# The chunked scan of a delta-rule attention with its operands and evictions laid out the other way round

## What is computed

```python
q, k, v = short_conv(x @ Wq.T), short_conv(x @ Wk.T), short_conv(x @ Wv.T)   # 4 taps, silu
q, k = l2norm(q), l2norm(k)
v, kb = v * beta, k * beta                 # chunks of 32 tokens, 8 a sequence
A = where(tri, 0, -kb @ k.T)               # T = inverse of (1 - A), row by row
u, w = T @ v, T @ kb
def step(S, (qi, ki, ui, wi)):             # over the 8 chunks in order
    attn = where(tri_s, 0, qi @ ki.T)
    u_i = ui - wi @ S
    o = qi @ S + attn @ u_i
    S = S + ki.T @ u_i
# paths = (3-tap filter of v, 63-tap filter of v, o, v); a small network on their
# means and variances gives softmax weights; out = norm(weighted sum) @ Wo.T
x = x + out
gate, value = x2 @ W11[e], x2 @ W12[e]     # x2 = layernorm(x), e over 8 experts
y = x + sum over the top 2 of score * ((gate * sigmoid(gate) * value) @ W2[e])
```

## Time and profile before

| what | number |
|---|---|
| median of the runs shown | 401.59 us (397.64 to 405.42, 3 runs) |
| the profiled execution | 399.36 us |
| its span | 397.5 us |
| TensorE busy (matmul) | 338.5 us, 85% |
| VectorE busy | 275.7 us, 69% |
| ScalarE busy | 139.4 us, 35% |
| GpSimd busy | 88.2 us, 22% |

### The profile page before, as it was taken

The page is one execution under the profiler, slowest core; times in us unless marked ns, Lnnn a source line. Parts: engine busy times, 40 slices in busy tenths (PEclk is TensorE's granted clock), DMA queues, the critical chain, the costliest instruction groups (busy, mean ns, idle before and its releaser), DMA issues.

```text
span 397.5 us, 14307 instructions
## 1 busy us (share of the span) xinstructions
PE 338.5 (85%) x6364; PEld 254.6 (64%) x6364; DVE 275.7 (69%) x679; ACT 139.4 (35%) x257; POOL 88.2 (22%) x152
## 2 busy tenths in 40 slices
PE   6989986966884679888989779989889999889997
PEld 6344974645433566755766557768767668668886
DVE  2889963256828874977765599779736969859654
ACT  2243614130352224354512613544252454242221
POOL 6463000061445234400201423702100000300000
PEclk9899889885597578999999998999989999978999
DMA  7331443001111011110000103020000000000000
GB/s 242 157 107 28 110 75 115 5 3 31 17 13 28 4 30 17 16 27 2 3 2 2 31 3 44 0 41 5 2 28 4 4 0 2 1 0 5 23 2 26
DMA packets 42668, 12.47 MB, mean 31 GB/s; under 512 B 35440, under 2 KB 41712, under 8 KB 42480
## 3 DMA queue, kind: packets, MB, share of 16 engines
q1 hardware_dynamic: 39440, 9.47, 11.1%
q10 hardware_dynamic: 3168, 2.10, 1.7%
HBM read 8.68 MB, written 2.88 MB: 29 GB/s over the span
## 4 chain that ended last, share of the span: by engine, by line
PE 60%; DVE 21%; issue 7%; ACT 5%; POOL 3%; DMA 2%; SPq 0%; DVEq 0%; ACTq 0%
PE ps L592 18%; PE ps L486 13%; PE ps L635 11%; PE ps L531 9%; PE ps L516 4%; DVE v_room L1266 2%; DMA late_sb<-in_late 2%; DVE x L1285 2%; POOL g L430 1%; PE ps L667 1%; PE ps L659 1%; PE ps L686 1%; DVE pmean L1317 1%; DVE toep_room L1318 1%; DVE toep_room L1369 1%
## 5 line engine op out<-in xcount | busy, mean ns | idle before, releaser
L635 PE MATMUL ps<-w_sb,v_room 128*128 128x128 f32 x512 | 64.3, 280 | 4.3 <-DVE v_room L1266 2.2
L635 PEld LDWEIGHTS ps<-w_sb,v_room 128*128 128x128 f32 x512 | 62.1, 195 | 8.8 <-DVE v_room L1266 4.3
L592 PE MATMUL ps<-x_hi,w_sb 128*128 128x512 f32 x128 | 61.0, 477 | 5.3 <-issue 1.9
L1266 DVE TENSOR_TENSOR v_room<-toep_room,ps 128x512 f32<-128x512 f32 x64 | 43.3, 682 | 30.3 <-PE ps L592 16.0
L885 ACT ACTIVATE toep_room<-ps 128x512 f32<-128x512 f32 x64 | 38.0, 596 | 66.1 <-PE ps L592 56.9
L592 PE MATMUL ps<-x_lo,w_sb 128*128 128x512 f32 x128 | 52.5, 410 | 0.0
L592 PE MATMUL ps<-x_hi,w_lo 128*128 128x512 f32 x128 | 52.4, 410 | 0.0
L1285 DVE SCALAR_TENSOR_TENSOR x<-ps,rs,x 128x128 f32<-128x128 f32 x128 | 35.9, 342 | 10.2 <-PE ps L635 9.9
L396 POOL TENSOR_TENSOR rn<-ss,mh 128x16 f32<-128x16 f32 x8 | 23.1, 2902 | 64.9 <-DVE ss L1106 64.9
L430 POOL TENSOR_TENSOR g<-gm,mh 128x16 f32<-128x16 f32 x4 | 11.6, 2906 | 105.5 <-DVE gm L1386 105.5
L592 PEld LDWEIGHTS ps<-x_hi,w_sb 128*128 128x128 f32 x128 | 25.1, 196 | 14.7 <-DVE v_room L1266 3.8
(11 more groups left out here) (202 smaller groups left out, 582.1 us busy)
## 6 DMA issues: line engine op xcount, KB each, us to landing
toep_room<-in_toep SPq DMA_DIRECT2D x1, 1536.0 KB, 12.6
a_d<-a_hc SPq DMA_DIRECT2D x4, 256.0 KB, 3.0
v_room<-in_w SPq DMA_DIRECT2D x1, 1024.0 KB, 5.7
t<-t_d SPq DMA_DIRECT2D x4, 256.0 KB, 3.0
v_room<-in_w ACTq DMA_DIRECT2D x1, 1024.0 KB, 6.1
taps_room<-in_taps SPq DMA_DIRECT2D x1, 768.0 KB, 6.3
x_sb<-in_x SPq DMA_DIRECT2D x1, 768.0 KB, 9.4
out_y<-x ACTq DMA_DIRECT2D x3, 256.0 KB, 2.4
```

The costliest lines, as they stand in the source:

```text
L592: ins = pe.matmul(bank[:, :], a[cols].bitcast(F32R), c[:, :].bitcast(F32R), start=(k == 0), stop=(k == 2))
L635: ins = pe.matmul(yb[:, P * j:P * j + P], fu[:, e % 2, f, P * j:P * j + P], w2_sb[:, FC * e + f, :], start=(f == 0), stop=(f == FC - 1))
L1266: dve.tensor_tensor(fu[:, e % 2, f, :], sg[:, i % 2, :], ps[VALUE[bank_of(p, i)]][:, :], ALU.mult).then_inc(s["fu_ready"], 1)
```

## The change

Every product of the scan is turned round, so that what was moving is stationary. Stationary are now vb, s_sb and u_sb, 32 columns each; the operands that went in as stationary are moving and lie side by side, so that one product serves several of them:

- vb against t32_t, 32 columns: the first part of u, transposed. It no longer waits for s_ready; that wait stands behind it.
- s_sb against by_s, 96 columns: wneg_t, q_t and a block named carry. carry is the 32 x 32 identity, so its 32 columns give s itself, transposed.
- u_sb against by_u, 64 columns: attn_t and kn, the output's second part and the state's new part.

The three results U, O and S of a step lie side by side in one bank, 96 columns for each of two sequences, and the bank alternates between ps2 and ps4. S is not added up over the scan in PSUM any more: every step adds the carried s and its new part.

The results come out transposed, so they are transposed as they leave PSUM. VectorE does that: a transpose of 128 x 64 in blocks of 32 x 32 for u (L1493 in the new numbering), one for s (L1498), and one for each step's output, straight into delta_hc (L1500). ScalarE's copies of u, s and delta are gone. VectorE's transposes of u and s stand between its lists, where ScalarE's copies stood between ScalarE's.

The identity block is made once at the start: VectorE folds the 128 x 128 identity to id32 and copies it 16 times into carry. In the tables, norm in list 6 of SCAN becomes norm_k in list 6, norm_q in list 7 and norm_kb in list 14, and the second weight split moves from list 0 of SCAN to the end of START. NEXT_START and NEXT_SCAN stay.

The core of the diff:

```diff
         [("q_silu", 0), ("q_hc", 0), ("qk_sq", 0), ("norms", 0)],
         [("router", 1), ("beta", 0), ("tanh", 0), ("beta_hc", 0), ("dstore", 0)],
         [("gate", 0), ("sig", 0), ("value", 0), ("fuse", 0)],
-        [("gate", 1), ("sig", 1), ("value", 1), ("fuse", 1), ("norm", 0), ("gate", 2)],
-        [("sig", 2), ("value", 2), ("gate", 3), ("fuse", 2)], [("g", 0), ("weigh", 0)], [("g", 1), ("mask", 0)],
+        [("gate", 1), ("sig", 1), ("value", 1), ("norm_k", 0), ("fuse", 1), ("gate", 2)],
+        [("sig", 2), ("value", 2), ("gate", 3), ("norm_q", 0), ("fuse", 2)], [("g", 0), ("weigh", 0)], [("g", 1), ("mask", 0)],
         [("sig", 3), ("value", 3), ("fuse", 3), ("centre", 0)],
         [("y", 0), ("square", 0), ("add", 0), ("centre", 3)], [("gate", 4), ("sig", 4), ("value", 4), ("spread", 0), ("fuse", 4)],
-        [("gate", 5), ("square", 3), ("sig", 5), ("value", 5), ("spread", 3)], [("fuse", 5)],
+        [("gate", 5), ("square", 3), ("sig", 5), ("value", 5), ("spread", 3)], [("fuse", 5), ("norm_kb", 0)],
         [("gate", 6), ("centre", 1), ("sig", 6), ("value", 6), ("square", 1)]]
 TAIL = [("delta", 0), ("centre", 2), ("spread", 1), ("square", 2), ("y", 1), ("gate", 7), ("sig", 7),
         ("value", 7), ("hidden_x", 0), ("spread", 2), ("stats", 0), ("fuse", 6), ("gate", 8), ("sig", 8),
...
     if rest and not any(what == "g" for what, _ in items):
         items.append(rest.pop(0))
 assert not rest
-START = [("split", 0), *START[:START.index(("y_out", 0)) + 1], ("reload", 0), *START[START.index(("y_out", 0)) + 1:]]
-SCAN[0].append(("split", 1))
+START = [("split", 0), *START[:START.index(("y_out", 0)) + 1], ("reload", 0), *START[START.index(("y_out", 0)) + 1:],
+         ("split", 1)]
 
 LAST_SCAN = [[item for item in items if item not in (("centre", 1), ("square", 1))] for items in SCAN]
 LAST_SCAN[13].append(("centre", 1))
...
         a_it, t_it, prod = sb("a_it", HB, HB), sb("t_it", HB, HB), sb("prod", HB * HB // 4)
         t16 = sb("t16", M, C)
 
-        kn, q_t, attn_t = (taps_room[:, TOK * k:TOK * k + TOK].rearrange("p (m c) -> p m c", c=C) for k in range(3))
+        by_u = taps_room[:, 0:2 * TOK].rearrange("p (m c) -> p m c", c=2 * C)
+        by_s = sb("by_s", M, 3 * C)
+        attn_t, kn = (by_u[:, :, C * k:C * k + C] for k in range(2))
+        wneg_t, q_t, carry = (by_s[:, :, C * k:C * k + C] for k in range(3))
+        id32 = sb("id32", C)
+
         vb = sb("vb", M, DH)
         t16_t, y_sb = sb("t16_t", M, C), sb("y_sb", M, C)
-        t32_t, wneg_t = sb("t32_t", M, C), sb("wneg_t", M, C)
+        t32_t = sb("t32_t", M, C)
         u_sb, s_sb = sb("u_sb", 2, DH), sb("s_sb", 2, DH)
         delta_hc = sb("delta_hc", M, DH)
         psq = sb("psq", NP, M, DH)
...
         ps = [ctx.enter_context(nc.psum_tensor(f"ps{i}", [P, 512], F32)) for i in range(8)]
         GATE, VALUE, YB, LAST_HALF = (5, 0), (6, 1), 7, 2
 
+        U_COL, O_COL, S_COL, COLS = 0, C, 2 * C, 3 * C
+
+        def scanned(n):
+
+            return ps[(2, 4)[n % 2]]
+
+        def slots(n, col):
+            return scanned(n)[:, 0:2 * COLS].rearrange("p (k c) -> p k c", k=2)[:, :, col:col + C]
+
         FIR = (2, 3, 5, 6)
 
 
...
                     if t is not None:
                         held()
                         if n == 0:
+                            pe.wait_ge(s["carry_ready"], 2)
                             pe.wait_ge(s["w_ready"], t1)
                             pe.wait_ge(s["vb_ready"], t1)
                             pe.wait_ge(s["moved"], t1)
-                        else:
-                            pe.wait_ge(s_ready[n - 1], t1)
                         for k in range(2):
                             m = k * NC + n
-                            ins = heads(ps[4], DH * k, DH, lambda q: t32_t[q, m, :], lambda q: vb[q, m, :],
-                                        start=True, stop=(n == 0))
-                            if n:
-                                ins = heads(ps[4], DH * k, DH, lambda q: wneg_t[q, m, :], lambda q: s_sb[q, k, :],
+                            ins = heads(scanned(n), COLS * k + U_COL, C, lambda q: vb[q, m, :], lambda q: t32_t[q, m, :],
+                                        start=(k == 0), stop=(n == 0))
+                        if n:
+                            pe.wait_ge(s_ready[n - 1], t1)
+                            for k in range(2):
+                                m = k * NC + n
+                                ins = heads(scanned(n), COLS * k, 3 * C, lambda q: s_sb[q, k, :], lambda q: by_s[q, m, :],
                                             start=False, stop=True)
                         ins.then_inc(s["u_done"], 1)
                     run(scan[2 * n])
                     if t is not None:
                         held()
                         pe.wait_ge(u_ready[n], t1)
-                        if n < NC - 1:
-                            for k in range(2):
-                                m = k * NC + n
-
-                                ins = heads(ps[3], DH * k, DH, lambda q: kn[q, m, :], lambda q: u_sb[q, k, :],
-                                            start=(n == 0 and k == 0), stop=(n == NC - 2))
-                            ins.then_inc(s["s_done"], 1)
                         for k in range(2):
                             m = k * NC + n
-                            if n:
-                                heads(ps[2], DH * m, DH, lambda q: q_t[q, m, :], lambda q: s_sb[q, k, :],
-                                      start=True, stop=False)
-                            ins = heads(ps[2], DH * m, DH, lambda q: attn_t[q, m, :], lambda q: u_sb[q, k, :],
-                                        start=(n == 0), stop=True)
-                        ins.then_inc(s["o_done"], 1)
+                            ins = heads(scanned(n), COLS * k + O_COL, 2 * C, lambda q: u_sb[q, k, :], lambda q: by_u[q, m, :],
+                                        start=False, stop=True)
+                        ins.then_inc(s["s_done"], 1)
                     run(scan[2 * n + 1])
                 run(behind)
 
...
-                def delta(_):
-                    if t is not None:
-                        act.wait_ge(s["o_done"], t * NC + NC)
-                        act.activation(delta_hc[:, :, :], ps[2][:, :].rearrange("p (m d) -> p m d", m=M),
-                                       ACT.Copy).then_inc(s["delta_ready"], 1)
-
...
                     return store(b)
                 ahead, scan, behind = lists(t)
                 run(ahead)
-                for n in range(NC):
-                    if t is not None:
-
-                        act.wait_ge(s["u_done"], t * NC + n + 1)
-                        if n:
-                            act.wait_ge(s["o_done"], t * NC + n)
-                        act.activation(u_sb[:, :, :], ps[4][:, 0:2 * DH].rearrange("p (b d) -> p b d", b=2),
-                                       ACT.Copy).then_inc(u_ready[n], 1)
-                    run(scan[2 * n])
-                    if t is not None and n < NC - 1:
-
-                        act.wait_ge(s["s_done"], t * (NC - 1) + n + 1)
-                        if n:
-                            act.wait_ge(s["o_done"], t * NC + n + 1)
-                        act.activation(s_sb[:, :, :], ps[3][:, 0:2 * DH].rearrange("p (b d) -> p b d", b=2),
-                                       ACT.Copy).then_inc(s_ready[n], 1)
-                    run(scan[2 * n + 1])
+                for items in scan:
+                    run(items)
                 run(behind)
 
             pipeline(body)
...
             for j in range(NT):
                 ins = dve.tensor_scalar(xn[:, j, :], x_sb[:, j, :], mv_first[:, j, 0:1], st[:, 2, j:j + 1], ALU.subtract, ALU.mult)
             ins.then_inc(s["xn_ready"], 1)
+            dve.wait_ge(s["pool_consts"], PADS_READY)
+            dve.tensor_reduce(id32[:, :], ident[:, :].rearrange("p (h j) -> p j h", h=H), AX.X, ALU.add).then_inc(s["carry_ready"], 1)
+            dve.wait_ge(s["carry_ready"], 1)
+            dve.tensor_copy(carry, id32[:, :].unsqueeze(1).to_broadcast([P, M, C])).then_inc(s["carry_ready"], 1)
             dve.wait_ge(s["early_loaded"], 32)
             dve.wait_ge(s["late_loaded"], 16)
             scaled(wkc, wk_sb, 1)
...
                     return run(ALONE)
                 ahead, scan, behind = lists(t)
                 run(ahead)
-                for items in scan:
-                    run(items)
+                for n in range(NC):
+                    if t is not None:
+                        dve.wait_ge(s["u_done"], t * NC + n + 1)
+                        dve.transpose(u_sb[:, :, :], slots(n, U_COL)).then_inc(u_ready[n], 1)
+                    run(scan[2 * n])
+                    if t is not None:
+                        dve.wait_ge(s["s_done"], t * NC + n + 1)
+                        if n < NC - 1:
+                            dve.transpose(s_sb[:, :, :], slots(n, S_COL)).then_inc(s_ready[n], 1)
```

(5 more changed lines are left out.)

12 lines of the change are left out of this document (6 added, 6 removed).

## The result

The changed kernel takes 426.4 us (median of 4 runs, 423.6 to 427.6) against 402.0 before: 1.0635 times as long, 95% interval 1.0528 to 1.0742. Forecast was 412 with a range to 420, so the direction was right and the size was about half.

The account below looks back on a forecast made before the run. In the scans TensorE and VectorE, both nearly full, were taken to share the limit. 5 + 5 + 2 + 1.7 - 1 = 12.7 us on 399.4 gave about 412; likeliest range 406 to 418, 8-in-10 range 395 to 420.

Parts of the forecast that it names:

- The order matters more than the price: In the scans, u, s and output wait behind whatever VectorE has queued, and TensorE behind them; transposes' own work 19 us.
- Price of a transpose, 0.21: Each 128x64 transpose on VectorE takes 0.21 us, ends 0.18 and 0.42; 92 of them add 19 us of work.
- Shorter products, 0.18 us a step: TensorE's middle scan step falls from 0.93 to 0.75 us, 5 us over 28 steps.
- the saving counts: Rival: VectorE reaches transposes in time, leaving shorter steps, fewer delta waits and one pause less: 389 us; chance 0.14.
- Scan 2, +5: Early transposes delay the normalisation and first fuse, some 2.9 us; s of step 4 behind the router's weights, about 2 more.
- Scan 4, +5: s of step 4 waits behind the router's weights until 308.1 at least; TensorE passes the last step some 6 us later.
- 13 transposes: Scan 4, weights to the long filter's centring: VectorE has no real pause, so these add 13 x 0.21 us.
- Scan 3, +2: Router's weights cost nothing as TensorE stood still; u of step 5 waits 0.84 us for masks, six late transposes cost more.
- Scan 1, +1.7: At its end the last u waits behind VectorE's variances and seven joining transposes, delaying the next pair's key convolutions 1.7 us.
- One pause fewer, -1: In the scans, a seventh fewer TensorE instructions removes one of the "issue" pauses of about 2 us, taken as -1.
- The clock as a rival: Rival: new waits lower the clock in scans 2 and 4, products grow 7 us: 419; chance 0.12, shared with dear transpose.
- a dear transpose: Rival: each VectorE transpose takes 0.42 us, 19 us more work, half on the path: 422; chance 0.12, shared with falling clock.

Follow-up runs that it names:

- the square of four: Ratios to the kernel before: its products with changed tables, ScalarE evicting 1.0011, VectorE evicting 1.064; turned products with ScalarE's copies 1.0003, with VectorE's transposes 1.0635.
- Both edits together: Changed kernel with router's weights cut in three, scan 2's beta and masks moved later, and useless products sized to the remaining waits: 414.0 us, ratio 1.0341.
- the kernel filled in scans 3 and 4: Changed kernel with ten useless products in TensorE's long waits of scans 3 and 4, none in scan 2: 418.4 us, ratio 1.0466.

## Why the prediction was half right

- **"The order matters more than the price": right**, and by the square of four shown as the whole of it. The Trainium skill ("TensorEngine Tiling (Array Packing)", section "PSUM Bottleneck") says to use both engines for evictions. For the scan alone that is not borne out: with all three evictions on ScalarE the turned products take 1.0003 times the kernel before, split over both engines 1.0313 and 1.0475, all on VectorE 1.0635. What counts here is whose list they stand in.
- **Price of a transpose, 0.21: nearly right.** 0.244, 0.246 and 0.212, together 21.5 us by durations instead of 19, and 14.5 in busy time.
- **Shorter products, 0.18 us a step: wrong.** 0.95 us, not 0.75. The prices for 64 and 96 columns, 14 and 21 ns, were right. What failed is the 12 ns of a narrow instruction: it is 8 ns, and the rest of the 0.93 us is mostly the 0.11 us on the way to a full-size product, twice a step, which stays in the turned step and which the sum left out. The rival "the saving counts" falls with it: the saving was not there to count. (Its ends, 8 us less and 2 more, also lie 3 and 7 from the 5 taken, not 3 either way.)
- **Scan 2, +5: mis-sized.** The scan lost 9.6 us (the part behind it took 0.7 back). Its first line held, the normalisation began at 142.53 where I said 142.1; but the first gate began 4.7 us late, where I had the first fuse 2.9 late, and behind the weights TensorE waited 2.85 us and in the next step another 1.96, where I had 2 in all.
- **Scan 4, +5: mis-sized.** s of step 4 came at 324.74; the forecast's 308.1 is 324.7 when counted from this scan's start, which lies 16.6 us later. What failed is the step behind that, the "13 transposes": I added their durations and took TensorE's own products to hide everything else. The waits show that ordinary pieces of VectorE are waited for as well, for some 16 us in the kernel: in scan 4 behind the weights 0.69 and 1.66 us. The slower products come on top. It lost 7.5 us.
- **Scan 3, +2: low** (3.3). The weights were said to cost nothing there, as TensorE stood still anyway. It waited 3.17 us, and the pause was gone: by the same products in both timelines 0.7 us net. The products right behind it, at a lower granted clock (0.50 against 0.69), lost 1.2 more. **Scan 1, +1.7: too high**; its last u came 0.3 us later.
- **One pause fewer, -1: wrong.** The pauses called "issue" ahead of the small products sum to 12.8 us, against 13.4 before. Two stand ahead of scan 4:

```profile
287.15 0.39 PE L606 MATMUL ps<-x_hi,w_lo 128*128 128x512 f32 x1 [1.34 <-issue]
...
291.11 0.24 PE L500 MATMUL ps<-t_t,kb 32*32 32x32 f32 x2 [2.13 <-issue]
```

  Before, the two there were shorter:

```profile
267.45 0.28 PE L486 MATMUL ps<-t,a_off_t 32*32 32x32 f32 x9 [1.21 <-issue]
...
276.67 0.59 PE L486 MATMUL ps<-t_t,kb 32*32 32x32 f32 x45 [0.52 <-issue]
```

  Behind the second the granted clock is 0.52; before, the whole part had 1.00. Together that part lost 4.0 us. Why they stand there is open; the kernel with turned products and ScalarE's copies lost 4.8 there and nothing in its total.
- **The clock as a rival: the wrong place for it.** I gave it 7 us *beside* the queue, and shared a chance of 0.12 between it and a dear transpose. It comes *with* the queue: behind the waits of 3.17 and 4.28 us the products ran at a granted clock of 0.50, and useless products in such waits gave 8 us back. 412 and 7 would have been 419, at the upper part of the range.

The failed step is thus the sum itself: each scan was priced by its long pieces, with ordinary ones hidden and the clock held fixed, and a pause was taken off. The terms +5, +5, +2, +1.7 and -1 for scans 2, 4, 3, 1 and the pause, 12.7 together, measured 9.6, 7.5, 3.3, 0.1 and, in the part ahead of scan 4, +4.0; small differences elsewhere make it 24.3. The direction was right, and for the reason given.

The causes behind the terms overlap and can't be added to 24: about 5 us are VectorE's work alone, 9 go with the order of its long pieces, 8 with filling the waits, each give or take 3 to 4. Both edits together gave 12, so about 5 would be counted twice, which is no more than that uncertainty. The last 12 us were not taken apart further than the 5 of work. That the other 7 are the waits that are left, the 22 short ones and the five filled ones, is argued from the waits, not shown by a run.

## What to carry to other kernels

Before an eviction in a recurrence is moved to another engine, count for each step what stands ahead of it in that engine's list, ordinary pieces too: here the other engine waited 10 us behind three long pieces and some 16 behind ordinary ones. The evictions' own work is the small part (about 5 of 24 us). Moving one of two evictions away did not halve the waits, the next one inherited them. When a forecast adds waits of 3 us and more to TensorE, add the slower products behind them to the same sum. And when small products are priced by a row, look at what follows them in the row: part of the time can belong to the change to the next kind of product.

## What the runs showed of the hardware that was not expected

- On 32 x 32 tiles, four heads at a time, an instruction costs 8 ns at 32 columns, 14 at 64 and 21 at 96, nearly in proportion, so putting operands side by side saves nothing by itself. Going over to a 128 x 128 product costs 0.11 us each time, whatever the columns (behind 32, 64 and 96 alike).
- The same pause need not give the same clock. The 1.92 us in the tail were followed by a granted clock of 0.53 in the changed kernel's profile and of 1.00 in that of the kernel filled in scans 3 and 4, ahead of the same products.
- The mean granted clock is no measure of time by itself. It rose from 0.914 to 0.948 in the kernel before with useless products, and to 1.00 in three scans with the turned products and ScalarE's copies, both for no gain; but in the changed kernel, where slow products stood on TensorE's own path, useless products were worth about 8 us.
